# Half of a scan's transposition moved from TensorE to VectorE: sixteen 32-partition block transposes per chunk, and a residual sum in two operations

## The reference

```
h = nan_to_num(take(embed_table, ids))                       # 64 x 256 x 256
x = layernorm(h)
f, i, g = sigmoid(x Wf'), sigmoid(x Wi'), max(x Wh' + 0.5, sigmoid(x Wh'))
s_t = f_t * s_(t-1) + i_t * g_t,  s_0 = 0.5                  # written in logs in the reference
h = h + s
x = layernorm(h)
r = relu(x W_fc' + gate * (x v' fast_b' u'))                  # W_fc, W_proj: ternary weights with a scale
out = h + (r * r) W_proj'
```

## Time and profile before

| | |
|---|---|
| Time, median of 3 runs | 965.42 us (964.8 to 967.37) |
| The profiled execution | 964.22 us, span 962.2 us, mean granted clock of TensorE 0.982 |
| Busy share of the span | PE 94%, ACT 82%, DVE 75%, POOL 44% |
| Products of L709 (the scan's transposes) | 256, 34.1 us by their durations |
| VectorE's longest waits | cand for ACT 52.2 us, h1 for the transposes 49.3 us, low for ACT 46.4 us, y_sb for PE 18.3 us |

### The profile page before, as it was taken

The page is one execution under the profiler, slowest core; times in us unless marked ns, Lnnn a source line. Parts: engine busy times, 40 slices in busy tenths (PEclk is TensorE's granted clock), DMA queues, the critical chain, the costliest instruction groups (busy, mean ns, idle before and its releaser), DMA issues.

```text
span 962.2 us, 17305 instructions
## 1 busy us (share of the span) xinstructions
PE 906.2 (94%) x5313; PEld 525.9 (55%) x5313; DVE 722.7 (75%) x1250; ACT 787.4 (82%) x1159; POOL 422.8 (44%) x459
## 2 busy tenths in 40 slices
PE   1577999999999999999999999999999999999986
PEld 1233656655566566555656665566566555655654
DVE  6677687877777878787777878777878787777663
ACT  4447788998888889888888998888889888888775
POOL 6542455544445554444455544445554444433110
PEclk8788999999999999999999999999999999999999
DMA  4211232122222212222222121223212222222210
GB/s 138 55 26 26 72 71 54 43 63 56 71 71 71 69 38 58 58 60 71 71 71 60 35 68 49 71 71 71 71 45 50 61 58 70 71 67 55 34 53 35
DMA packets 161754, 57.91 MB, mean 60 GB/s; under 512 B 140358, under 2 KB 160400, under 8 KB 161728
## 3 DMA queue, kind: packets, MB, share of 16 engines
q1 hardware_dynamic: 155584, 53.38, 22.7%
q0 software_dynamic: 6144, 4.21, 1.9%
HBM read 19.81 MB, written 16.78 MB: 38 GB/s over the span
## 4 chain that ended last, share of the span: by engine, by line
PE 88%; ACT 4%; DVE 3%; DMA 2%; issue 1%; SPq 1%; POOL 0%; ACTq 0%; DVEq 0%
PE bank L652 33%; PE y_ps L626 22%; PE bank L696 21%; PE bank L700 5%; PE turned L709 3%; PE bank L610 3%; ACT normed L391 1%; DMA x_cols<-x_rows 1%; DMA sq<-w_fc 1%; ACT relu L438 1%; ACT x_rows L398 1%; SPq L257 0%; ACT sq L451 0%; ACT sq L371 0%; DVE hid L983 0%
## 5 line engine op out<-in xcount | busy, mean ns | idle before, releaser
L696 PE MATMUL bank<-x_cols,fc_t 128*128 128x512 f16 x1024 | 263.7, 380 | 0.7 <-issue 0.7
L652 PE MATMUL bank<-x_cols,w_hi 128*128 128x512 f16 x768 | 231.1, 383 | 22.2 <-DMA x_cols<-x_rows 19.4
L321 POOL TENSOR_SCALAR var_eps<-moments 128x4 f32<-128x4 f32 x64 | 60.5, 945 | 420.8 <-DVE moments L784 420.8
L652 PE MATMUL bank<-x_cols,w_lo 128*128 128x512 f16 x768 | 231.1, 383 | 0.0
L626 PE MATMUL y_ps<-proj_t,sq_hi 128*128 128x256 bf16 x1024 | 225.5, 273 | 2.7 <-DVE sq_lo L931 2.5
L626 PE MATMUL y_ps<-proj_t,sq_lo 128*128 128x256 bf16 x1024 | 225.5, 273 | 0.0
L438 ACT ACTIVATE relu<-bank,relu_scale 128x512 f32<-128x512 f32 x256 | 165.7, 690 | 13.7 <-PE bank L700 13.7
L311 POOL DMA_INDIRECT rows_raw<-table,idx_now x128 | 148.4, 1159 | 59.5 <-issue 31.0
L696 PEld LDWEIGHTS bank<-x_cols,fc_t 128*128 128x128 bf16 x1024 | 100.2, 98 | 114.2 <-issue 1.5
L931 DVE TENSOR_TENSOR sq_lo<-sq,sq_hi 128x1024 f16<-128x1024 f32 x128 | 150.5, 1215 | 12.1 <-ACT sq L451 12.0
L391 ACT ACTIVATE normed<-h,shift,rstd 128x256 f32<-128x256 f32 x256 | 132.7, 597 | 17.3 <-POOL shift L329 16.7
(11 more groups left out here) (131 smaller groups left out, 942.2 us busy)
## 6 DMA issues: line engine op xcount, KB each, us to landing
out<-out_sb SPq DMA_DIRECT2D x32, 512.0 KB, 3.2
rows_raw<-table,idx_now POOLq DMA_INDIRECT x128, 2.6
x_cols<-x_rows SPq DMA_TRANSPOSE x128, 2.7
sq<-w_fc SPq DMA_DIRECT2D x1, 1024.0 KB, 7.2
pj_raw<-w_proj SPq DMA_DIRECT2D x1, 1024.0 KB, 9.4
w_raw<-wf SPq DMA_DIRECT2D x1, 256.0 KB, 2.7
w_raw<-wi SPq DMA_DIRECT2D x1, 256.0 KB, 2.9
w_raw<-wh SPq DMA_DIRECT2D x1, 256.0 KB, 3.9
```

Source lines behind the costliest of these rows:

```text
L652: ins = pe.matmul(bank[gate_bank[p]][:, :], w[:, k, q, :], x_part(0, par, part)[:, :, k, :], start=(k == 0 and w is w_hi and part == 0), s ...
L696: pe.matmul(dst[:, :], fc_t[:, k, f * P:(f + 1) * P], x_part(1, 0, part)[:, :, k, :], start=(k == 0 and part == 0), stop=False)
```

## The change

The transposition of the half e = 0 is taken from TensorE. VectorE transposes `hid[:, 0, :]` in blocks of 32x32: for each of four groups i of 32 source partitions and each of four groups q of 32 target partitions one instruction with 32 partitions and 4 x 32 elements (one block of each of the four token tiles), which writes a new SBUF tile `hid_rows`. Eight of the sixteen stand behind `scan(0)`, eight behind `guard`. TensorE keeps the four transposes of e = 1. The residual sum becomes two operations of 4 x 128 elements, from `hid_rows` and from `turned`. On SP `store(n-2)` moves behind `turn_rows(0, n+1)`. The setup tile `pj_a` now lies on `out_sb`'s memory.

```diff
@@ sync engine, step
-                if not isinstance(n, int) or n > 1:
-                    store(n - 2, par)
                 if known_below(n, N - 1):
                     wait(sp, gate_done, 6 * n)
                     pass_on(sp, sp_passed, n)
                     turn_rows(0, n + 1, 1 - par)
+                if not isinstance(n, int) or n > 1:
+                    store(n - 2, par)
@@ TensorE, step
                         for j in range(TILES):
-                            for e in range(KD):
-                                ins = pe.transpose(turned_rows[:, j, e * P:(e + 1) * P],
-                                                   hid[:, e, j * P:(j + 1) * P], ident[:, :])
+                            ins = pe.transpose(turned_rows[:, j, P:D], hid[:, 1, j * P:(j + 1) * P], ident[:, :])
                         ins.then_inc(hid_turned, 1)
@@ VectorE, step
                 def scan(e):
                     dve.wait_ge(value_ready, 2 * n + e + 1)
-                    wait(dve, hid_turned, n)
+                    if e == 0:
+                        wait(dve, blocks_ready, B * B * n)
+                    else:
+                        wait(dve, hid_turned, n)
...
+                def turn_blocks(parts):
+
+                    dve.wait_ge(scanned, 4 * n + 2)
+                    wait(dve, h1_low, n)
+                    for i in parts:
+                        from_block = hid[BLOCK * i:BLOCK * (i + 1), 0, :].rearrange("r (j q c) -> r j q c", j=TILES, q=B)
+                        for q in range(B):
+                            dve.transpose(hid_rows[BLOCK * q:BLOCK * (q + 1), :, BLOCK * i:BLOCK * (i + 1)],
+                                          from_block[:, :, q, :]).then_inc(blocks_ready, 1)
...
                     scan(0)
+                    turn_blocks(range(2))
...
                 if front:
+                    turn_blocks(range(2, B))
+                    dve.wait_ge(blocks_ready, B * B * (n + 1))
+                    dve.tensor_tensor(h1[:, par, :, 0:P], hid_rows[:, :, :], h0[:, par, :, 0:P], ALU.add)\
+                        .then_inc(h1_low, 1)
                     dve.wait_ge(hid_turned, n + 1)
-                    dve.tensor_tensor(h1[:, par, :, :], turned_rows, h0[:, par, :, :], ALU.add).then_inc(h1_ready, 1)
+                    dve.tensor_tensor(h1[:, par, :, P:D], turned_rows[:, :, P:D], h0[:, par, :, P:D], ALU.add)\
+                        .then_inc(h1_ready, 1)
+                    dve.wait_ge(h1_low, n + 1)
                     dve.wait_ge(h1_ready, n + 1)
                     measure(1, n, h1[:, par, :, :])
```

More of the change, by code:

```diff
@@ L44 @@
 RELU_TOP = 2.0 ** 6
+BLOCK = 32
+B = P // BLOCK
 FIRST_LOOP, LAST_LOOP = 5, N - 4
@@ L93, in build @@
         hid = sb("hid", [P, KD, CHUNK])
+        hid_rows = sb("hid_rows", [P, TILES, P])
         low = sb("low", [P, CHUNK], F16)
@@ L114, in build @@
         pj_raw = sb("pj_raw", [P, KD, HID])
-        pj_a = sb("pj_a", [P, KD, HID])
+        pj_a = out_sb[:, :, :, :].rearrange("p a j d -> p a (j d)")
         pj_s = sb("pj_s", [P, 3, KD])
@@ L195, in build @@
         hid_turned = sem("hid_turned")
+        blocks_ready = sem("blocks_ready")
+        h1_low = sem("h1_low")
         h1_ready = sem("h1_ready")
```

## The result

The changed kernel takes 1021.22 us (median of 4 runs, 1020.76 to 1023.28), the kernel before 965.11 beside it: a ratio of 1.0584, 95% interval 1.0556 to 1.0611. It is slower by 56 us. The forecast was 1030, the range 985 to 1068.

A forecast was written before the change was run, and what follows sets the result against it. TensorE bounds the kernel before; with the change the ring through VectorE does, at 23.77 + 0.5 + 16 x 0.34 = 29.7 us. 91.97 + 10.9 + 30 x 29.7 - 2.4 + 37.0 = 1028, adjusted to 1030 us; range 985 to 1068.

The forecast's parts named there:

- The beat before is TensorE's: Steady steps of the kernel before: TensorE sets the 27.72 us step; four fewer transposes would make it 27.28 us.
- the ring: Loop from h1's moments through GpSimd, ScalarE and VectorE back to the moments: 23.77 us before, 29.7 us with the change.
- 3.95 us of slack: VectorE's waits per step from `cand` to the moments' end, on engines keeping TensorE's beat; they vanish if VectorE is late.
- Sixteen transposes at 0.34 us: VectorE from `cand` to moments: 0.30 us each plus 0.04 for lost overlap, start to start; 5.44 us a step.
- The loss of overlap: VectorE: where partitions change, as with each transpose's target, the next operation starts 0.04 us after the last one's end.
- The rival with s = 0.20: VectorE transposes overlap, s being the distance of their starts in us: ring 27.5 us, time 958, faster; chance 0.10.
- the formula 856 + 512 s: Whole kernel: approximate time in us for a distance s between the starts of VectorE's transposes.
- 0.5 us of waits and the second sum: VectorE around the transposes: waits for its own results, a two-operation sum and two-counter statistics add 0.5 us to the ring.
- The first steps: First two steps, where the chain runs through VectorE too: 32 transposes put 10.9 us straight on the end.
- TensorE waits for low: TensorE's L705, formerly L700, should wait for VectorE's `low` about 2.4 us a step, some 70 us in all.
- TensorE's busy time falls by 14 to 17 us: TensorE over the whole changed kernel: sign expected in the profile, busy time lower by 14 to 17 us.
- SP and pj_a cost nothing: SP's new order leaves the gate transfers 7 us of cover; `pj_a`'s last setup reader comes before the first emit; no cost.

The follow-up runs named there:

- run 3: Changed kernel without VectorE's sixteen transposes, the first sum reading hid as it lies; TensorE keeps four transposes: 955.38 us, ratio 0.9868 to the kernel before.
- run 5: Changed kernel with ScalarE's first four gate evictions of a step ahead of the normalisation of h1: 994.62 us, ratio 1.0292 to the kernel before.
- run 6: Changed kernel with guard moved from ahead of the second eight transposes to behind the moments of h1: 993.61 us, ratio 1.0301 to the kernel before.
- run 1: Changed kernel with each VectorE transpose reading and writing the same group of 32 partitions, results not in place: 970.41 us, ratio 1.0038 to the kernel before.
- run 2: Changed kernel with the transposes reordered so four in a row keep the target group and only the source's changes: 1022.89 us, ratio 1.0567 to the kernel before.
- Run 7: Changed kernel with SP's old order, the store ahead of the transfers for the next gates: 1021.79 us, ratio 1.0573 to the kernel before.

## Why the prediction was right, step by step

*The beat before is TensorE's, and the ring has 3.95 us of slack.* Confirmed: with the transposes left out the step falls to 27.28 us (run 3), and with all sixteen it is the ring's. VectorE at 75% busy was right to be called nearly full; runs 5 and 6 show that the place of the work in the ring counts and not its total, since each gained about 1 us a step with VectorE's work unchanged. The distance from the moments to `cand`, forecast to stay near 10.2 us, is 10.31 and 10.19.

*Sixteen transposes at 0.34 us.* Measured 0.335. The price of one, taken as 0.30 from elementwise rows of 284 and 293 ns, is 0.303 with its group change and 0.26 without. That it came out to 1% is partly luck: no row of before had a transpose, and the rows it was taken from are of operations that overlap. The loss of overlap, taken from one gap of 0.04 us behind `low`, was the step on which the sign hung, and run 1 shows it: 0.207 us from start to start without the change, and 970 instead of 1021. The rival with s = 0.20 had 958. At an average of 0.225 (each source group still begins with a held one) the formula 856 + 512 s gives 971, and 970.4 was measured; at the changed kernel's 0.335 the same formula gives 1027.5, 6 us more than measured, so the agreement to 1 us is partly chance. The statement of the Trainium skill's page "VectorE: DVE Perf Modes", section "Two Vector instructions with no wait between them", that a start in another group of 32 partitions on either side makes an instruction wait for all earlier ones, agrees with runs 1 and 2.

*0.5 us of waits and the second sum.* Too much: the step is 29.46, and 29.46 - 23.77 - 5.36 leaves 0.33. Of the terms, the waits for VectorE's own results were too dear: 0.15 us was put on each, as ahead of the moments, and the transposes start 0.03 us behind the scan (557.46 to 557.49) and the sum 0.03 behind the last transpose (569.36 to 569.39). The second sum and the statistics cost more than the few hundredths left for them: from the first sum to the moments it is 3.08 us (569.39 to 572.47) instead of 2.82 (561.78 to 564.60). In the sum of the prediction the 30 steps had 886.6 us and took 981.74 - 101.40 = 880.3, 6 us less, the largest part of the 9 by which 1030 is too high.

*The first steps.* 10.9 us were put on them; the moments of step 1 came 9.4 us later (101.40 against 91.97), while VectorE's waits up to there fell from 19.2 to 17.9 us, so that they absorbed most of the difference. The end behind the last moments took 37.9 us instead of 37.0.

*TensorE waits for low.* The first place is right, the size not: 49.1 us in 30 waits, 1.6 a step instead of 2.4. The prediction had one place too few. Of the 2.18 us that a step is longer than 27.28, 1.6 are this wait, 0.16 to 0.17 the overlap that the product behind it loses, and 0.29 the projection's wait for the third `sq_lo`, as the starts above show for the step of 29.62 us; for the one of 29.30 they add up likewise (a wait of 1.57).

*TensorE's busy time falls by 14 to 17 us.* It did not: 905.3 against 906.2. In run 3, where TensorE has no such waits, it is 896.3, 10 us less. At each of the two late places a product is shown without a neighbour's overlap, 0.16 us more, which in 30 steps makes 9.6 us and covers the difference of the two.

*SP and pj_a cost nothing.* Run 7 confirms it for SP's order. For `pj_a` there is no run, so that it costs nothing is not shown; the setup shows no wait on it.

## What to carry to other kernels

A busy share tells little of how much an engine can take over: follow the ring of waits that passes through it, take out the waits on engines that keep the present beat, and compare what is left with that beat. Here an engine at 75% had 4 us in 27.7 to give, and the work cost 5.4. The small VectorE transposes here that hop between groups of 32 partitions lost their overlap; one instruction over all partitions, with the hops left to transfers that have time, cost 0.7 us for the same blocks. And when such a ring binds, reordering alone can shorten it: two moves that left all work in place gave 27 us each, of the second some 11 (0.38 a step) by a GpSimd chain that got shorter, which was not forecast.

## What the runs showed of the hardware that was not expected

- On TensorE a transpose of 64 partitions costs no less than one of 128: four behind four full ones add 0.48 us to the distance of starts (0.92 instead of 0.44 us), and four full ones cost 0.44.
- GpSimd's small operations last differently with what VectorE does beside them. The reciprocal root of four numbers takes 1.87 us behind the moments of h1 and 1.04 behind those of h0 in both kernels, and in run 6 1.87 and 1.86; var_eps takes 0.46 us beside `guard` and 0.91 beside `guard_sum`. What of VectorE's operations does it, no run here separates.
